# Order of VectorE's pieces inside an attention round: key counts, key shift and loser flags placed later or earlier

## The chip, the cores and the metric

The kernel runs on one core of one Trainium2 chip. The metric is the device time in microseconds of one execution, taken as the median of several runs. It is one transformer layer: attention with top-k pruning, then a mixture-of-experts part.

## The reference, cut to what matters

```python
mod = (silu(c) @ wmod).reshape(4, 6, 1, -1)            # sa, ca, ga, sb, cb, gb; ga and gb kept away from 0
h = layernorm(x) * (1 + ca) + sa                       # x: (4, 1024, 256)
q, k, v = (keep_largest(h @ w.T) for w in (wq, wk, wv))  # 16 heads of 16; of 16 features only the largest |.| stays
s = q @ k.T / 4, causal                                # per head, 1024 x 1024
s = keep the 64 largest of each row, the others -inf (ties: the lower key first)
x = x + ga * (softmax(s) @ v) @ wo.T
h = layernorm(x) * (1 + cb) + sb
g = softmax(h @ router_w + router_b)                   # 8 experts, each takes its 512 best tokens
x = x + gb * sum over experts of (relu(tok @ w1 + b1) @ w2 + b2) * g
```

Since only one feature of a query and one of a key survives, a score is a single product. Which keys belong to the 64 largest can be told by counting: `left` counts, along the keys, how many with the same feature and sign have gone by, and a row's kept keys are found by comparing ranks with counts.

## The kernel before, in words

The attention part goes in 16 **rounds** (`for gi in range(GA)`), each one batch `b` and one group `g` of four heads. A round's scores are computed in nine **units** (`UNITS`), each a piece of the 1024 x 1024 plane for four heads. TensorE computes `scores(gi, u)` (L424, L430, L435) into a ring of three pairs of PSUM banks (`begin`, `f_free`), ScalarE takes the exponential (`exps`, L947) into `p_buf`, and TensorE multiplies with the values (`pv`, L457) into PSUM bank 6. Bank 7 (`m_begin`, `f_mfree`) is used in turn by small results: turned key and query rows (`rows`, L376), `zero_rank` (L384 to L386), `own_key` (L392), `lost` (L400, L401), turned outputs (`turn_back`, L504), modulation rows (L517). Each of them waits until the one before has been emptied.

Units 1 and 4 hold the first 128 keys, among which the last of the 64 kept ones are decided: TensorE computes `chosen` (L448, L451) into two further ring buffers, and VectorE compares, `mask(gi, c, a)` (L1280), which needs the unit's exponentials and frees the ring buffer. `scores(gi, 5)` needs the buffer of `mask(gi, 1, 0)`.

In every round but the last, VectorE also prepares the next round's (`n = gi + 1`) keys and queries:

- `key_counts(n)` (L1221, L1223): which keys are zero, and the scan over all 1024 keys; it releases TensorE's `zero_rank(n)` by `f_cnr`.
- `keys(n)` (L1231 to L1244): the running maximum of the keys, their marks, the largest key `k_max` (L1241), and last the keys shifted by it (L1243, L1244), which releases `own_key(n)` by `f_kp`.
- `queries(n)` (L1249 to L1251), releases `lost(n)` by `f_uq`.
- `zero_rank(n)` (L1256, L1259), `losers(n)` (L1266), `negatives(n)` (L1272) empty bank 7 after TensorE's `zero_rank`, `own_key` and `lost`.

Other pieces on VectorE are `out_rows_of` (L1285 to L1288, divides the outputs and empties bank 7), and the next batch's work: `norm_stats` (L1168), `normalize` (L1178), `modulate` (L1188) and, four times in each round with g of 1 or 2 of the first three batches (`tiles`: rounds 1, 2, 5, 6, 9, 10), `one_feature` (L1198, L1203), which ScalarE's `evict_y` (L921) feeds and GpSimd's `keep` (L789, L790) follows; `feature_limits` (L1208 to L1215) in rounds 3, 7, 11. The batch before is finished in the next batch's rounds: `gate_weights`, `take_weights`, `take_mod`, `residual` (g = 0), `second_norm` (rounds 7, 11, 13). GpSimd further does `stage` (L769) and `tri` (L779, the triangle of units 2, 3 and 8, which `pv` of these units waits for).

The order on every engine is written out by hand, and each engine works its list strictly in order. So a piece that waits holds back all behind it. VectorE's order in a round stands in the loop at the end of its block (L1421 to L1494); TensorE's, ScalarE's and GpSimd's in theirs.

Of the kernel before, what the change touches and what calls it, by code (L numbers as in the profile page):

```python
# [32 lines left out]
def build_kernel(nc, x, wq, wk, wv, wo, router_w, router_b, w1, b1, w2, b2, c, wmod, out):  # L33
    with ExitStack() as ctx:
# [74 lines left out]
        def sf(name, shape, dt=F32):  # L109
            return fst.enter_context(nc.sbuf_tensor(name, shape, dt))  # L110
# [38 lines left out]
        kd = sf("kd", [P, 2, T])  # L149
# [89 lines left out]
        def full_of(u):  # L239
            return f_full[ring_at[u] % 3], ring_at[u] // 3 + 1  # L240
# [7 lines left out]
        def p_of(gi, u):  # L248
            return p_buf[:, (NU * gi + u) % PB]
# [34 lines left out]
        with nc.Block() as blk:  # L284
# [762 lines left out]
            def _(dve):  # L1047
# [133 lines left out]
                def modulate(b, half):  # L1181
                    u = ("T", b, half)
                    dve.wait_ge(*full_of(u))
                    v = ("Y", b - 1, NT - 1 if b > 1 else 3) if half == 0 else ("Y", b, 3)
                    if b:
                        dve.wait_ge(*full_of(v))
                    for k in range(KD):
                        m = dve.tensor_scalar(h_of(b, half)[:, k, :], buf(u)[:, k, :], mod_t[:, 1, k, b:b + 1], mod_t[:, 0, k, b:b + 1],  # L1188
                                              ALU.mult, ALU.add)
                    dve.drain().then_inc(free_of(u)[0], 1)  # L1190
                    dve.nop().then_inc(f_hT, 1)
                    dve.nop().then_inc(f_xfree, 1)

                def one_feature(b, t):
                    i = NT * b + t
                    dve.wait_ge(f_yev, i + 1)
                    y_abs, y_val, y_one = y_of(b, t)
                    dve.tensor_reduce(y_mx[:, b % 2, t, :], y_abs, AX.X, ALU.max)  # L1198
                    dve.drain()
                    if y_turn(b, t) > 0:  # L1200
                        dve.wait_ge(f_keep, y_turn(b, t))
                        dve.wait_ge(f_cnt, y_turn(b, t))
                    dve.tensor_tensor(y_one, y_abs,  # L1203
                                      y_mx[:, b % 2, t, :].unsqueeze(2).to_broadcast([P, 3 * NH, HD]),
                                      ALU.is_equal).then_inc(f_one, 1)
# [21 lines left out]
                def keys(n):  # L1227
                    par = n % 2
                    kx = kd[:, par, :]

                    dve.tensor_tensor_scan(mx[:, :], kx[:, 0:512], kx[:, 0:512], 0.0, ALU.max, ALU.max)  # L1231
                    dve.tensor_reduce(k_max1[:, :], kx[:, 512:T], AX.X, ALU.max)
                    dve.tensor_scalar(k_far[:, :], k_not[:, :], -FAR, None, ALU.mult)
                    dve.tensor_tensor(n_lo[:, :], n_lo[:, :], left[:, T - 1:T], ALU.min)
                    dve.scalar_tensor_tensor(kb[:, :], k_not[:, 0:P], FAR, kx[:, 0:P], ALU.mult, ALU.add)
                    dve.scalar_tensor_tensor(k_one[:, :, :], kx[:, 0:P].unsqueeze(1).to_broadcast([P, HG, P]), 0.0,
                                             onesz[:, :, :], ALU.is_gt, ALU.mult)
                    dve.scalar_tensor_tensor(k_opp[:, :, :], ks[:, par, :].unsqueeze(1).to_broadcast([P, HG, P]), 0.0,
                                             onesz[:, :, :], ALU.is_lt, ALU.mult)
                    dve.drain()  # L1240
                    dve.tensor_tensor(k_max[:, :], mx[:, 511:512], k_max1[:, :], ALU.max)  # L1241
                    dve.drain()
                    dve.tensor_scalar(ks[:, par, :], ks[:, par, :], k_max[:, :], None, ALU.subtract)  # L1243
                    dve.scalar_tensor_tensor(kx, kx, k_max[:, :], k_far[:, :], ALU.subtract, ALU.add).then_inc(f_kp, 1)  # L1244
# [30 lines left out]
                def mask(gi, c, a):  # L1275
                    u = ("Z", gi, c, a)
                    dve.wait_ge(*free_of(("S", gi, FIRST[c], a)))
                    dve.wait_ge(*full_of(u))
                    pb = p_of(gi, FIRST[c])[:, 2 * a:2 * a + 2, :]
                    dve.scalar_tensor_tensor(pb, buf(u), 1.0, pb, ALU.is_gt, ALU.mult).then_inc(free_of(u)[0], 1)  # L1280

                def out_rows_of(gi, c):
                    m_full(("O", gi, c))
                    o4 = ps[:, 7, :].rearrange("p (q h d) -> p q h d", q=4, h=HG)
                    dve.tensor_tensor(z_lo[:, :, :], z_lo[:, :, :], o4[:, :, :, HD], ALU.min)  # L1285
                    dve.reciprocal(o_inv[:, :, :], o4[:, :, :, HD])
                    dve.drain()
                    dve.tensor_tensor(o_tok[:, 4 * c:4 * c + 4, heads(gi % NG), :], o4[:, :, :, 0:HD],  # L1288
                                      o_inv[:, :, :].unsqueeze(3).to_broadcast([P, 4, HG, HD]), ALU.mult).then_inc(f_mfree, 1)
                    if gi % NG == NG - 1:  # L1290
                        dve.drain().then_inc(f_otok, 1)
# [129 lines left out]
                for gi in range(GA):  # L1421
                    b, g = divmod(gi, NG)
                    n = gi + 1
                    more, pre, post = n < GA, b + 1 < B, b > 0
                    tiles = pre and g in (1, 2)
                    t0 = 4 * (g - 1)

                    if g == 0 and post:
                        gate_weights(b - 1)
                        take_weights(b - 1)  # L1430
                    if gi == GA - 1:
                        gate_weights(b)
                        take_weights(b)
                    mask(gi, 0, 0)
                    mask(gi, 0, 1)
                    if gi == 0:
                        router_constants()
                        feature_limits(0)
                        finish_mod()
                    if tiles:  # L1440
                        one_feature(b + 1, t0)
                    if g == 0 and pre:
                        norm_stats(b + 1, 0)
                    if post and g == norm_group(b - 1):
                        second_norm(b - 1, 0)
                    if gi:
                        out_rows_of(gi - 1, 1)
                    if more:
                        key_counts(n)
                    if g == 0 and pre:  # L1450
                        normalize(b + 1, 0)
                    if tiles:
                        one_feature(b + 1, t0 + 1)
                    mask(gi, 1, 0)
                    mask(gi, 1, 1)
                    if post and g == norm_group(b - 1):
                        second_norm(b - 1, 1)
                    if g == 1 and pre:
                        norm_stats(b + 1, 1)
                    if more:  # L1460
                        keys(n)
                    if tiles:
                        one_feature(b + 1, t0 + 2)
                    out_rows_of(gi, 0)
                    if g == 0 and post:
                        take_mod(b - 1)
                    if gi == GA - 1:
                        take_mod(b)
                    if more:
                        queries(n)  # L1470
                    if g == 0 and post:
                        residual(b - 1, 0)
                    if more:
                        zero_rank(n)
                    if g == 1 and pre:
                        normalize(b + 1, 1)
                    if g == 0 and pre:
                        modulate(b + 1, 0)
                    if tiles:
                        one_feature(b + 1, t0 + 3)  # L1480
                    if g == 3 and pre:
                        feature_limits(b + 1)
                    if more:
                        losers(n)
                    if g == 0 and post:
                        residual(b - 1, 1)
                    if g == 1 and pre:
                        modulate(b + 1, 1)
                    if post and g == norm_group(b - 1):
                        router_max(b - 1, (0, 1))  # L1490
                    if more:
                        negatives(n)
                    if post and g == norm_group(b - 1):
                        router_share(b - 1, (0, 1))  # L1494
# [761 lines left out]
```

## Time and profile before

| | |
|---|---|
| median of 3 runs | 1086.58 us (1085.47 to 1089.87) |
| profiled execution, its own time | 1082.71 us |
| its span | 1080.8 us |
| TensorE matmul busy | 918.9 us (85%) |
| VectorE busy | 660.8 us (61%) |
| ScalarE busy | 480.0 us (44%) |
| GpSimd busy | 272.0 us (25%) |
| mean granted TensorE clock | 0.916 |

The span runs from the first to the last instruction; the execution's own time has 1.9 us around it. The attention rounds lie between about 65 us and 740 us, the experts behind them. The rows further down are from timelines: start, duration, engine, line, operation, tiles, count, and in brackets how long the engine had been idle before and what ended it. Rows of one kind that follow each other are merged, so that the duration is that of the whole run of them.

### The profile page before, as it was taken

Reading aid. Unit: us, or ns where it says so; the run is one execution under the profiler, and the core shown is the slowest. Engines: PE = TensorE matmul, PEld = TensorE weight load, DVE = VectorE, ACT = ScalarE, POOL = GpSimd, SP = SyncE. Lnnn points to the kernel's source line nnn. Section 1 sums busy time; section 2 is a strip of 40 time slices with the busy share of each in tenths; the row PEclk is TensorE's granted clock in tenths of the full one; section 3 lists DMA queues with packets and bytes.
Section 4 is the critical chain, followed back from the end, with each engine's and each line's share of the span. In section 5 each row is a group of like instructions: output and inputs, shape, how many; then the busy total and the mean of one; then the engine's idle time right before and its main releaser. Section 6 shows DMA issues by size and latency. Waiting matters only on the chain. (4 is left out here: it accounts for less than half of the span.)

```text
span 1080.8 us, 17735 instructions
## 1 busy us (share of the span) xinstructions
PE 918.9 (85%) x6760; PEld 503.2 (47%) x6760; DVE 660.8 (61%) x1454; ACT 480.0 (44%) x631; POOL 272.0 (25%) x404
## 2 busy tenths in 40 slices
PE   6778999888999888999989999985015999999995
PEld 4533444344444453544435535334003766666664
DVE  6757767566678657586684683634685455543441
ACT  2635667663667745476765475551000122222110
POOL 3503222321222402232221200010004333334222
PEclk9779999999999989999998998996555999999998
DMA  4000000000100011100002102001822134442111
GB/s 153 4 1 21 1 21 2 1 1 1 60 20 1 1 47 34 60 1 2 2 1 80 38 4 80 1 20 40 294 99 54 39 107 115 107 113 40 20 20 20
DMA packets 34856, 46.60 MB, mean 43 GB/s; under 512 B 2184, under 2 KB 30928, under 8 KB 34640
## 3 DMA queue, kind: packets, MB, share of 16 engines
q1 hardware_dynamic: 28624, 36.89, 10.2%
q0 software_dynamic: 6144, 8.52, 4.9%
q8 instruction: 57, 0.93, 0.4%
q14 instruction: 31, 0.25, 0.1%
HBM read 32.69 MB, written 12.72 MB: 42 GB/s over the span
## 5 line engine op out<-in xcount | busy, mean ns | idle before, releaser
L947 ACT ACTIVATE p_buf<-ps 128x1024 f32<-128x1024 f32 x288 | 279.4, 1023 | 181.0 <-PE ps L424 96.5
L424 PE MATMUL ps<-qx,kd 32*128 32x512 f32 (+3 forms) x1280 | 146.8, 535 | 29.8 <-DVE p_buf L1280 26.1
L457 PE MATMUL ps<-p_buf,vv 128*17 128x512 f32 (+3 forms) x1664 | 156.3, 477 | 0.0
L2089 ACT ACTIVATE h_t<-ps,b_t 128x512 f32<-128x512 f32 x64 | 44.0, 687 | 247.6 <-PE ps L2029 247.6
L1280 DVE SCALAR_TENSOR_TENSOR p_buf<-ps,p_buf 128x1024 f32<-128x1024 f32 x64 | 76.7, 1220 | 76.7 <-ACT p_buf L947 63.7
L2029 PE MATMUL ps<-tok_t,w_sb 128*128 128x512 f32 x256 | 113.8, 603 | 0.0
L2039 PE MATMUL ps<-w_sb,h_t 128*128 128x256 f32 x512 | 112.5, 380 | 0.8 <-ACT h_t L2089 0.8
L779 POOL TENSOR_SCALAR_AFFINE_SELECT p_buf<-p_buf 128x512 f32<-128x512 f32 x64 | 42.0, 670 | 272.4 <-ACT p_buf L947 269.7
L2039 PEld LDWEIGHTS ps<-w_sb,h_t 128*128 128x128 f32 x512 | 96.6, 190 | 15.3 <-ACT h_t L2089 1.6
L424 PEld LDWEIGHTS ps<-qx,kd 32*128 32x128 f32 x1280 | 55.1, 191 | 71.7 <-issue 56.2
L365 PE MATMUL ps<-w_t,h_t 128*128 128x512 f32 (+1 forms) x224 | 78.8, 496 | 0.8 <-ACT w_t L889 0.8
L789 POOL TENSOR_TENSOR qk<-y_val,y_one 128x512 f32<-128x512 f32 x28 | 32.4, 1159 | 179.2 <-DVE y_one L1203 179.2
L2029 PEld LDWEIGHTS ps<-tok_t,w_sb 128*128 128x128 f32 x256 | 49.0, 193 | 59.0 <-issue 58.7
L1988 POOL DMA_INDIRECT out_dram<-ctr,ids x32 | 50.8, 1587 | 95.9 <-issue 95.9
L457 PEld LDWEIGHTS ps<-p_buf,vv 128*17 128x17 f32 x1664 | 34.3, 97 | 60.3 <-issue 46.2
L365 PEld LDWEIGHTS ps<-w_t,h_t 128*128 128x128 f32 x224 | 40.4, 190 | 40.8 <-issue 39.3
L2141 DVE TENSOR_TENSOR eo<-ps,b_sb 128x256 f32<-128x256 f32 x32 | 13.6, 425 | 72.1 <-PE ps L2039 68.6
L921 ACT ACTIVATE y_abs<-ps 128x768 f32<-128x768 f32 x28 | 22.7, 811 | 47.9 <-PE ps L365 45.9
L2127 DVE SCALAR_TENSOR_TENSOR gbk<-gb_sb,of_b,gbk 128x256 f32<-128x256 f32 x96 | 40.1, 480 | 1.8
L1977 POOL DMA_INDIRECT tok<-h_table,ids x32 | 35.2, 1099 | 23.2 <-issue 22.0
L1198 DVE TENSOR_REDUCE y_mx<-y_abs 128x48 f32<-128x768 f32 x28 | 26.7, 952 | 22.9 <-ACT y_abs L921 22.6
L1223 DVE TENSOR_TENSOR_SCAN left<-k_not,minus 128x1024 bf16<-128x1024 bf16 x15 | 39.8, 2656 | 1.1
(291 smaller groups left out, 1406.2 us busy)
## 6 DMA issues: line engine op xcount, KB each, us to landing
w_sb<-in_L_ffn_w_dram SPq DMA_DIRECT2D x16, 1024.0 KB, 9.0
h_table<-xr SPq DMA_DIRECT2D x3, 1056.0 KB, 4.6
x_in<-in_L_attn_x_dram SPq DMA_DIRECT2D x6, 512.0 KB, 4.0
out_dram<-xr SPq DMA_DIRECT2D x3, 1024.0 KB, 5.2
xr<-in_L_attn_x_dram SPq DMA_DIRECT2D x3, 1024.0 KB, 5.7
h_table<-xr SPq DMA_DIRECT2D x2, 528.0 KB, 3.1
xr<-in_L_attn_x_dram SPq DMA_DIRECT2D x2, 512.0 KB, 5.4
p_buf<-in_L_wmod_dram SPq DMA_DIRECT2D x1, 1024.0 KB, 8.8
```

Of the source, the lines that this page charges most:

```text
L365: m = pe.matmul(buf(u)[:, bank, 0:n], src[:, k, (t % 4) * P:(t % 4 + 1) * P], w_t[:, k, lo:lo + n], start=k == 0, stop=k == KD - 1)
L424: m = pe.matmul(o, key, qx[r, par, t0:t0 + w], start=True, stop=not early)
L457: m = pe.matmul(ps[32 * h:32 * h + HD + 1, 6, o:o + w], vv[:, (gi // NG) % 2, i, HG * (gi % NG) + h, :], p_of(gi, u)[:, h, lo:lo + w], sta ...
L779: m = pool.affine_select(p, p, [[0, HG], [1, P]], ALU.is_ge, 0.0, base=0, channel_multiplier=-1)
L947: act.activation(p_of(gi, u)[:, 2 * a:2 * a + 2, :], buf(w), ACT.Exp, scale=0.25).then_inc(free_of(w)[0], 1)
L1223: dve.tensor_tensor_scan(left[:, :], k_not[:, :], minus1[:, :].to_broadcast([P, T]), TOPK + 0.5, ALU.add, ALU.add)
L1280: dve.scalar_tensor_tensor(pb, buf(u), 1.0, pb, ALU.is_gt, ALU.mult).then_inc(free_of(u)[0], 1)
L1988: pool.indirect_dma_start(out_rows, bass.IndirectOffsetOnAxis(ids[:, e, k:k + 1], 0), ctr[:, e % 2, k, :], None, compute_op=ALU.add).then_ ...
L2029: m = pe.matmul(ps[:, L1_BANKS[f % 3], :], w1_sb[:, e % WB, k, f * P:(f + 1) * P], tok_t[:, e % 2, k, :], start=k == 0, stop=k == KD - 1)
L2039: m = pe.matmul(ps[:, 4 + q % 2, 0:D], h1_t[:, f, q * P:(q + 1) * P], w2_sb[:, e % WB, f, :], start=f == 0, stop=f == FO - 1)
L2089: act.activation(h1_t[:, f, :], ps[:, L1_BANKS[f % 3], :], ACT.Relu, bias=b1_t[:, e * FO + f:e * FO + f + 1]).then_inc(s_h1, 1)
L2127: dve.scalar_tensor_tensor(gbk[:, a, q, :], gb_sb[:, b, :], of_b[:, e, q, b:b + 1], gbk[:, a, q, :], ALU.mult, ALU.add)
```

## The change

Only the order of VectorE's list changes. `keys(n)` is cut in two: its last two instructions (with the drain before them) become `keys_shifted(n)`. `key_counts(n)` and `normalize(b + 1, 0)` now stand behind the second `one_feature` and the two comparisons of unit 4; `out_rows_of(gi, 0)` stands between `keys(n)` and `keys_shifted(n)`, and ahead of the third `one_feature`; `losers(n)` stands ahead of the fourth `one_feature` and of `feature_limits`.

```diff
@@ def keys(n)
                     dve.drain()
                     dve.tensor_tensor(k_max[:, :], mx[:, 511:512], k_max1[:, :], ALU.max)
+
+                def keys_shifted(n):
+                    par = n % 2
+                    kx = kd[:, par, :]
                     dve.drain()
                     dve.tensor_scalar(ks[:, par, :], ks[:, par, :], k_max[:, :], None, ALU.subtract)
                     dve.scalar_tensor_tensor(kx, kx, k_max[:, :], k_far[:, :], ALU.subtract, ALU.add).then_inc(f_kp, 1)
@@ the loop over the rounds
                     if gi:
                         out_rows_of(gi - 1, 1)
+                    if tiles:
+                        one_feature(b + 1, t0 + 1)
+                    mask(gi, 1, 0)
+                    mask(gi, 1, 1)
                     if more:
                         key_counts(n)
                     if g == 0 and pre:
                         normalize(b + 1, 0)
-                    if tiles:
-                        one_feature(b + 1, t0 + 1)
-                    mask(gi, 1, 0)
-                    mask(gi, 1, 1)
                     if post and g == norm_group(b - 1):
                         second_norm(b - 1, 1)
                     if g == 1 and pre:
                         norm_stats(b + 1, 1)
                     if more:
                         keys(n)
+                    out_rows_of(gi, 0)
+                    if more:
+                        keys_shifted(n)
                     if tiles:
                         one_feature(b + 1, t0 + 2)
-                    out_rows_of(gi, 0)
...
                     if g == 0 and pre:
                         modulate(b + 1, 0)
+                    if more:
+                        losers(n)
                     if tiles:
                         one_feature(b + 1, t0 + 3)
                     if g == 3 and pre:
                         feature_limits(b + 1)
-                    if more:
-                        losers(n)
```

## Rows read from the trace of the kernel before

**Rows 1.** The page, busy time of TensorE: us, share, instructions.

```profile
PE   918.9 (85%) x6760; PEld 503.2 (47%) x6760; DVE 660.8 (61%) x1454; ACT 480.0 (44%) x631; POOL 272.0 (25%) x404
```

**Rows 2.** Sums of waits: who waited for whom, us in total, times, longest.

```profile
PE ps L424 <- DVE p_buf L1280: 26.1, 16, 3.9
```

**Rows 3.** Timeline of TensorE in round 3 (rank products, scores of unit 5, bank-7 steps).

```profile
207.11 0.89 PE L448 MATMUL ps<-uq,wk_r 32*128 32x512 bf16 x4
...
210.20 1.14 PE L424 MATMUL ps<-qx,kd 32*128 32x512 f32 x8 [1.61 <-DVE p_buf L1280]
...
217.31 0.23 PE L384 MATMUL ps<-left,partner 128*128 128x128 bf16 x1 [0.25 <-DVE o_tok L1288]
...
219.89 1.16 PE L392 MATMUL ps<-kb,k_one 128*128 128x128 f32 x8 [0.18 <-DVE z_rank L1256]
...
223.18 0.23 PE L400 MATMUL ps<-upto,lw 128*128 128x128 bf16 x1 [1.16 <-DVE lw L1266]
```

**Rows 4.** Timeline of ScalarE in round 3, exponentials of unit 4.

```profile
206.53 1.94 ACT L947 ACTIVATE p_buf<-ps 128x1024 f32<-128x1024 f32 x2 [0.80 <-PE ps L424]
```

**Rows 5.** Timeline of VectorE in round 3.

```profile
204.42 0.17 DVE L1285 TENSOR_TENSOR z_lo<-z_lo,ps 128x16 f32<-128x16 f32 x1 [3.75 <-PE ps L504]
...
205.17 0.68 DVE L1221 TENSOR_SCALAR k_not<-kd 128x1024 bf16<-128x1024 f32 x1
205.93 2.72 DVE L1223 TENSOR_TENSOR_SCAN left<-k_not,minus 128x1024 bf16<-128x1024 bf16 x1
208.83 2.36 DVE L1280 SCALAR_TENSOR_TENSOR p_buf<-ps,p_buf 128x1024 f32<-128x1024 f32 x2 [0.19 <-issue]
211.10 1.22 DVE L1231 TENSOR_TENSOR_SCAN mx<-kd 128x512 f32<-128x512 f32 x1
...
215.02 0.29 DVE L1243 TENSOR_SCALAR ks<-ks,k_max 128x128 f32<-128x128 f32 x1
...
216.42 0.16 DVE L1285 TENSOR_TENSOR z_lo<-z_lo,ps 128x16 f32<-128x16 f32 x1
...
217.40 0.75 DVE L1249 SCALAR_TENSOR_TENSOR qm<-mx,k_max,qx 128x512 bf16<-128x512 f32 x1
...
219.54 0.29 DVE L1256 TENSOR_SCALAR z_rank<-ps 128x128 f32<-128x128 f32 x1
...
220.80 0.36 DVE L1208 TENSOR_REDUCE y_ext<-y_mx 128x1 f32<-128x256 f32 x1
...
222.00 1.13 DVE L1266 SCALAR_TENSOR_TENSOR lw<-ps,y_mx,tie 128x128 bf16<-128x128 f32 x4
```

**Rows 6.** Timeline of VectorE in round 14, `losers`.

```profile
689.13 1.13 DVE L1266 SCALAR_TENSOR_TENSOR lw<-ps,y_mx,tie 128x128 bf16<-128x128 f32 x4 [1.33 <-PE ps L392]
```

**Rows 7.** Timeline of VectorE in round 1, second `one_feature` and the comparisons.

```profile
123.99 0.95 DVE L1198 TENSOR_REDUCE y_mx<-y_abs 128x48 f32<-128x768 f32 x1 [0.38 <-ACT y_abs L921]
...
125.96 2.35 DVE L1280 SCALAR_TENSOR_TENSOR p_buf<-ps,p_buf 128x1024 f32<-128x1024 f32 x2
```

**Rows 8.** Timelines at the end of round 2: GpSimd's triangle, TensorE's unit 8 products.

```profile
193.90 1.22 POOL L779 TENSOR_SCALAR_AFFINE_SELECT p_buf<-p_buf 128x512 f32<-128x512 f32 x2
...
196.82 1.06 PE L457 MATMUL ps<-p_buf,vv 128*17 128x384 f32 x16
```

**Rows 9.** Timelines: `normalize` in rounds 1 and 4, TensorE's waits in round 4.

```profile
142.68 1.28 DVE L1178 TENSOR_SCALAR x_in<-x_in,mv,rstd 128x256 f32<-128x256 f32 x4
...
241.65 2.28 DVE L1178 TENSOR_SCALAR x_in<-x_in,mv,rstd 128x256 f32<-128x256 f32 x4
...
246.34 1.54 PE L424 MATMUL ps<-qx,kd 32*128 32x512 f32 x8 [3.91 <-DVE p_buf L1280]
...
254.68 1.12 PE L517 MATMUL ps<-mod_rows,pick_b 4*128 4x512 f32 x2
```

**Rows 10.** Busy time by stretch: engines' us, TensorE's granted clock behind POOL's.

```profile
127.00:131.00 4.00, 3.67 (x16) 1.31 (x20) 3.85 (x12) 2.17 (x3) 1.52 (x3) 0.57 0.00 0
```

## The prediction

> **What bounds the kernel now.** I read the busy times, then the sums of waits, then the timelines of TensorE, VectorE, ScalarE and GpSimd through the sixteen rounds (a round is one pass of `for gi in range(GA)`: one batch, four heads). TensorE is busy 918.9 us of 1080.8 [rows 1], so in the attention part an edit counts only through what TensorE waits for. The wait to be attacked is plain: `scores(gi, 5)` needs the ring buffer that unit 4's comparison `mask(gi, 1, 0)` frees, and over 16 rounds it cost 26.1 us [rows 2]. Round 3 shows why. TensorE began the rank products at 207.11 and the next scores only at 210.20, 1.61 us idle [rows 3]; ScalarE's exponentials of unit 4 began at 206.53, two in 1.94 us [rows 4]. VectorE had run `key_counts` from 205.17 and could compare only at 208.83 [rows 5]. So the comparison was 1.2 us late (it could have run at about 207.6, when the first exponential and the first rank product are there).
>
> The same rows show a second thing. After the comparison VectorE works without a hole from 208.83 to 223.1, and in this stretch TensorE stops three more times for it: `zero_rank` at 217.31, `own_key` at 219.89, `lost` at 223.18 (1.16 us idle) [rows 3, 5]. They use one PSUM bank in turn, so each waits for VectorE to empty the one before. The late half of a round is VectorE's; the early half has its holes, 3.75 us in front of `out_rows_of(gi-1, 1)` among them [rows 5].
>
> **The change, part by part.** No instruction is added or removed and no DMA is moved; SP's and GpSimd's own lists stay. Only VectorE's order changes.
>
> (a) `key_counts` goes behind the two comparisons. It takes 3.5 us (205.17 to 208.65, two instructions and two drains) [rows 5]. Before, 2.3 to 3 us of it filled time in which VectorE would have waited for the comparison; now those stay empty and all 3.5 us lie in the busy half. The comparison comes 1.2 us sooner, the work behind it is 3.5 us longer.
>
> (b) The two shifting instructions go behind `out_rows_of(gi, 0)`. They take 1.4 us (215.02 to 216.42), the output rows 0.9 [rows 5]. Hence `zero_rank` on TensorE is spared these 1.4 us, but `own_key` needs `queries` and VectorE's `zero_rank` behind both, and gains nothing.
>
> (c) `losers` goes ahead of the fourth `one_feature` and of `feature_limits`. This takes 1.2 us (220.80 to 222.00) out of the path to `lost` in rounds 3, 7 and 11 [rows 5], and 1.97 us (123.99 to 125.96, one `one_feature` [rows 7]) in the six tile rounds.
>
> Now by round, measured at `lost`, the last thing TensorE needs of VectorE in a round.
>
> *Round 3.* Comparisons 207.65 to 210.0, counts to 213.5, keys (3.9, from 211.10 to 215.02) to 217.4, output rows to 218.1: `zero_rank` at 218.15 instead of 217.31. Shift to 219.6, queries (2.1) to 221.9, rank out 222.2: `own_key` at 222.25 instead of 219.89, +2.36. It takes 1.1, `losers` 1.1 more, `lost` at about 224.6 instead of 223.18: **+1.4**. `feature_limits` is then behind it, and there is time: TensorE is in the next unit 0.
> *Rounds 7 and 11* are alike with the second normalisation in between: **+1.2** each. *Round 13* has no `feature_limits` to move: **+2.35**. *Round 14* likewise, but there `losers` had waited 1.33 us for `own_key` [rows 6], which absorbs half: **+1.25**. Together 7.4.
>
> *Rounds 1, 5, 9* (features and the other half's statistics). Here the comparison is held by the second `one_feature`, which waits for ScalarE (0.38 us idle, 123.99) [rows 7], so taking the counts away frees nothing: the 0.72 us wait in these six rounds stays. The path to `lost` becomes 3.5 longer by (a) and 1.97 shorter by (c), 1.5; taken as **+1.45** each, since in round 5 `lost` waited a shade for this path already. Together 4.35.
>
> *Rounds 2, 6, 10.* VectorE has 2 to 3 us of holes behind the comparison, so `lost` moves by −0.3 to +0.35. But the fourth `one_feature` now comes 2.7 to 3.3 us later, and behind it GpSimd has `keep`, `stage` and the triangle of unit 8, which ended at 195.12, 1.7 us before TensorE's products of unit 8 at 196.82 [rows 8]. The cover of 1.7 us is gone and 1.0 to 1.3 are late: **+1.05, +1.65, +1.65**, 4.35.
>
> *Round 0.* The wait of 3.06 us shrinks, the counts and `normalize` stand behind. **+1.2**, with `normalize` at 1.2 us. In front of the comparison it took 2.28 for its four tiles in round 4 and only 1.28 in round 1 [rows 9]; in the slow one GpSimd was copying (`stage`), in the fast one not, and at its new place it is not. If it kept 2.28, rounds 0, 4 and 8 would each be 1.1 worse. The Trainium skill (GPSIMD Engine Reference, 1. Specifications) says that GpSimd shares its SBUF interface with VectorE's two-port and two-input instructions; by that rule the moved piece gets faster, and the rows agree.
>
> *Rounds 4 and 8.* TensorE waits 3.91 us here [rows 9]: counts and `normalize` both in front. TensorE could go on 3.4 us sooner (the rest of the 3.91 is the comparison itself). Then the fetch of the modulation rows waits for `out_rows_of(gi, 0)`: comparisons to 242.8, counts 246.3, normalising 247.5, keys 251.4, output rows 252.1, against 254.68 [rows 9]. Behind that, projection and residual give the pace as before: **−2.5** each, −5.
> *Round 12* has no `normalize`; its modulation rows come at the same time, **0**; round 15 has none of the moved pieces, 0.
>
> Sum: 7.4 + 4.35 + 4.35 + 1.2 − 5 = **+12.3 us**.
>
> (d) The clock, the one term the trace doesn't show for the new order. After the wait of round 1 TensorE's mean grant over 127 to 131 was 0.57, the 1.2 GHz level, for 3.4 us [rows 10]; I count one behind this wait in eight of the sixteen rounds (the scores there take up to twice as long: 1.54 in round 4 against 1.14 in round 3 [rows 3, 9]). One costs half its length, 1.7 us, unless TensorE waits for VectorE anyway. My sum hides them behind VectorE's path. Bounds: 0 (all stay hidden), and 11 rounds × 1.7 = +18.7 (in each of the 11 rounds that get longer, the new waits make one in the open). I take one more in the open, +1.7, because most new waits are followed at once by another that would cover it. The Trainium skill (TensorE: Matmul & The Clock Gate, Part 1) has the gate follow how busy the array has lately been; by that rule waits moved from one place to two in a round are no better than one, which speaks against the change.
>
> So **+14 us**: 1082.71 + 14 = 1096.7 for an execution like the profiled one. The three runs have their median at 1086.58, 3.9 above the profiled execution, and I give the time against it: **1100.6 us**.
>
> **The rivals.**
> 1. *Forecast*: VectorE's busy half grows by the counts and TensorE loses there more than it wins at unit 4. For it: three waits in that half already. Chance 0.60.
> 2. *The clock in the open*: as 1, with low stretches behind most `zero_rank` and `own_key` waits: +12.3 and 8 to 18.7, 1107 to 1117. Against it: the wait of 1.61 us in round 3 brought no low stretch (the eight products behind it took 1.14 us in all [rows 3]). By the Trainium skill's rule on the gate, cited above, this would be the outcome. Chance 0.18.
> 3. *It wins* (the other side): the comparison sits on the path of every round and the late half has room that I overlook, so the waits are simply gone: 2.6 in round 0, 1.2 in five rounds, 3.4 in rounds 4 and 8, 1.3 in round 12, 16.7 us less, 1070. It decides if `own_key` in round 3 comes no later than 11.1 us after the comparison's start, which it does now (208.83 to 219.89) [rows 3, 5]. Against it: that distance is filled with VectorE's work already. Chance 0.10.
> 4. *A wash*: moving `losers` and the output rows ahead gives back what the counts cost, because `lost` and not `own_key` is what TensorE needs; the six tile rounds then cost nothing and the sum is about +3.5. 1086 to 1092. Chance 0.12.
>
> **How the numbers follow.** About 0.5%, 5.4 us, is what a measurement of this kernel can tell from no change. Cases 1 and 2 are slower (0.78), 3 is faster (0.10), 4 the same (0.12). The range goes from the upper half of the wash, 1089, to the middle of the clock's case, 1113.
>
> **What would show it.** Right: the wait of `scores` for L1280 falls from 26.1 to about 10 us; new waits of L384 (2 to 4 us in rounds 0, 3, 4, 7) and L392 (1 to 2 us in most rounds); in rounds 2, 6 and 10 TensorE's unit 8 products wait for GpSimd about 1 us; rounds 4 and 8 shorter. Wrong: L392 without waits, or VectorE with holes between comparison and `losers` in the plain rounds; or low-clock stretches behind the new waits in most rounds (then case 2).

## The result: 1.4% slower, and the profile after

| | before | after |
|---|---|---|
| median | 1087.55 us (1085.47 to 1089.87) | 1102.93 us (1100.37 to 1104.32) |
| profiled execution, its own time | 1082.71 us | 1104.06 us |
| its span | 1080.8 us | 1102.2 us |

Four runs of each; ratio 1.0139, interval 1.0113 to 1.0166. The medians lie 15.4 us apart, the two profiled executions 21.4: the one of before was 4.8 us under the median of its runs and faster than each of them, the one after 1.1 us over its own. So what is read from the two traces below is up to 6 us larger than what the medians show. Slower executions of the kernel before have the lower mean grant (1079.91 us at 0.917, 1089.24 us at 0.907). The lines of before are now 4 higher from L1243 on: comparison L1284, output rows L1289 to L1292, shift L1247 and L1248, `zero_rank` L1260, `losers` L1270.

The page of the kernel after, busy times, to hold against [rows 1]:

```profile
PE 925.6 (84%) x6760; PEld 507.7 (46%) x6760; DVE 655.5 (59%) x1454; ACT 481.6 (44%) x631; POOL 264.4 (24%) x404
```

The instructions are the same. TensorE needs 6.7 us more for its own (925.6 instead of 918.9), so more of them ran at the low clock; the rest of the 21.4 us went into waits. Sums of waits of the kernel after, TensorE, 65 to 765 us (total, times, longest), against [rows 2]:

```profile
PE ps L384 <- DVE o_tok L1292: 19.0, 9, 3.2
PE ps L392 <- DVE z_rank L1260: 15.0, 10, 2.1
PE ps L424 <- DVE p_buf L1284: 9.5, 16, 1.1
PE ps L517 <- DVE o_tok L1292: 4.9, 3, 2.1
PE ps L457 <- POOL p_buf L779: 3.1, 3, 1.0
```

The wait that was attacked fell from 26.1 to 9.5 us. In its place stand 15.0 at `own_key`, where there had been 0.5, 19.0 at `zero_rank` instead of 4.7, 4.9 at the modulation rows and 3.1 at GpSimd's triangle. Round 3 shows how, TensorE's timeline of the kernel after, against [rows 3]:

```profile
215.86 0.89 PE L448 MATMUL ps<-uq,wk_r 32*128 32x512 bf16 x4
217.73 1.14 PE L424 MATMUL ps<-qx,kd 32*128 32x512 f32 x8 [0.39 <-DVE p_buf L1284]
...
226.45 0.23 PE L384 MATMUL ps<-left,partner 128*128 128x128 bf16 x1 [1.87 <-DVE o_tok L1292]
...
230.46 2.08 PE L392 MATMUL ps<-kb,k_one 128*128 128x128 f32 x8 [0.67 <-DVE z_rank L1260]
...
234.31 0.29 PE L400 MATMUL ps<-upto,lw 128*128 128x128 bf16 x1
```

VectorE's timeline of the same round, kernel after, against [rows 5]:

```profile
213.17 0.17 DVE L1289 TENSOR_TENSOR z_lo<-z_lo,ps 128x16 f32<-128x16 f32 x1 [3.75 <-PE ps L504]
...
216.36 2.36 DVE L1284 SCALAR_TENSOR_TENSOR p_buf<-ps,p_buf 128x1024 f32<-128x1024 f32 x2 [2.35 <-ACT p_buf L947]
218.63 0.68 DVE L1221 TENSOR_SCALAR k_not<-kd 128x1024 bf16<-128x1024 f32 x1
219.39 2.29 DVE L1223 TENSOR_TENSOR_SCAN left<-k_not,minus 128x1024 bf16<-128x1024 bf16 x1
221.80 1.23 DVE L1231 TENSOR_TENSOR_SCAN mx<-kd 128x512 f32<-128x512 f32 x1
```

VectorE now idles 2.35 us in front of the comparison, where it had counted before, and has the counts between comparison and keys. From the comparison's start to `zero_rank` it is 10.1 us (forecast 10.5, before 8.5), to `own_key` 14.1 (forecast 14.6, before 11.1), to `lost` 17.95 (before 14.35; forecast 16.95).

Read at `lost` (from one round's to the next, after minus before):

| rounds | forecast | measured |
|---|---|---|
| 0 | +1.2 | +2.3 |
| 3, 7, 11, 13, 14 | +7.4 | +10.7 |
| 1, 5, 9 | +4.35 | +8.5 |
| 2, 6, 10 | +4.35 | +4.3 |
| 4, 8 | −5 | −1.75 |
| 12 | 0 | −1.8 |
| sum | +12.3 | +22.2 |

Two things have to be known for this table. TensorE's waits for the triangle, 1.05 us each, which the forecast counts in rounds 2, 6 and 10, stand behind `lost` (in round 2 at 205.58, `lost` at 198.11), so the table has them a round later. Put where the forecast has them, the second row is +7.6 measured against +7.4, and the fourth +7.4 against +4.35. And 1.3 of the +2.3 in round 0 lie in front of everything that was moved (last section).

### The profile page after: what moved, and what is told of

It reads as the page before. It is cut to its first block and busy times, and to the rows that moved or that the text cites. A ratio compares the mean times of both kernels' runs of the same rounds, so it can differ in the third digit from the quotient of the medians.

```text
span 1102.2 us, 17735 instructions
## 1 busy us (share of the span) xinstructions
PE 925.6 (84%) x6760; PEld 507.7 (46%) x6760; DVE 655.5 (59%) x1454; ACT 481.6 (44%) x631; POOL 264.4 (24%) x404
## 5 line engine op out<-in xcount | busy, mean ns | idle before, releaser
L457 PE MATMUL ps<-p_buf,vv 128*17 128x512 f32 (+3 forms) x1664 | 158.5, 482 | 3.1 <-POOL p_buf L779 3.1
L1284 DVE SCALAR_TENSOR_TENSOR p_buf<-ps,p_buf 128x1024 f32<-128x1024 f32 x64 | 76.8, 1222 | 97.3 <-ACT p_buf L947 82.1
L789 POOL TENSOR_TENSOR qk<-y_val,y_one 128x512 f32<-128x512 f32 x28 | 35.1, 1254 | 186.2 <-DVE y_one L1203 186.2
L457 PEld LDWEIGHTS ps<-p_buf,vv 128*17 128x17 f32 x1664 | 34.2, 97 | 60.3 <-issue 43.1
L424 PE MATMUL ps<-qx,ks 32*128 32x512 f32 x256 | 37.4, 654 | 3.9 <-ACT p_buf L947 3.9
```

The lines of the kernel that those rows point to most:

```text
L424: m = pe.matmul(o, key, qx[r, par, t0:t0 + w], start=True, stop=not early)
L457: m = pe.matmul(ps[32 * h:32 * h + HD + 1, 6, o:o + w], vv[:, (gi // NG) % 2, i, HG * (gi % NG) + h, :], p_of(gi, u)[:, h, lo:lo + w], sta ...
L789: pool.tensor_tensor(qk[:, t], y_val[:, 0:2 * NH], y_one[:, 0:2 * NH], ALU.mult)
```

## The experiments

A ratio is always to the kernel before on the same chip, with its interval. The chips differ a little (the kernel before took 1082.35 us on one and 1087.55 on another), so runs are compared by their ratios. All runs return the same result as the kernel before.

### The moves one by one

**Counts and normalising alone.** The kernel before, with this edit only:

```diff
-                    if more:
-                        key_counts(n)
-                    if g == 0 and pre:
-                        normalize(b + 1, 0)
...
                     mask(gi, 1, 1)
+                    if more:
+                        key_counts(n)
+                    if g == 0 and pre:
+                        normalize(b + 1, 0)
```

> Part (a) alone: key_counts and normalize behind the comparisons of unit 4, output rows and losers where they were before. Theory (the counts' 3.5 us lie in VectorE's busy half): slower than the changed kernel, since (b) and (c) had paid part of it back: lost comes 1.2 us later in rounds 3, 7 and 11, up to 2 us later in rounds 1, 5 and 9, about 0.4 in rounds 2, 6 and 10, and output rows 1.5 us later in rounds 4 and 8; about 1116 us, 13 us over the changed kernel. Rival (the loss is low-clock stretches, the order behind the comparisons doesn't matter): within 4 us of the changed kernel, 1099 to 1107.

Measured: 1132.49 us, ratio 1.0409 (1.0364 to 1.0454). The direction is the theory's, the size is not: 46 us lost instead of 29. Sums of waits, TensorE:

```profile
PE ps L384 <- DVE o_tok L1288: 40.5, 12, 4.7
PE ps L517 <- DVE o_tok L1288: 9.6, 3, 3.6
PE ps L424 <- DVE p_buf L1280: 9.5, 16, 1.1
```

The comparison's wait is 9.5 here too, so this gain comes from this piece alone; and nothing waits at `own_key`. The loss stands at `zero_rank`, in waits of up to 4.7 us.

**Output rows ahead of the shift, and `losers` earlier, alone.** The kernel before, with `keys` cut in two as in the change, and with these edits only:

```diff
                         keys(n)
+                    out_rows_of(gi, 0)
+                    if more:
+                        keys_shifted(n)
                     if tiles:
                         one_feature(b + 1, t0 + 2)
-                    out_rows_of(gi, 0)
...
+                    if more:
+                        losers(n)
                     if tiles:
                         one_feature(b + 1, t0 + 3)
                     if g == 3 and pre:
                         feature_limits(b + 1)
-                    if more:
-                        losers(n)
```

> Parts (b) and (c) alone: the output rows ahead of the key shift, losers ahead of the fourth one_feature and feature_limits; key_counts and normalize stay in front of the comparisons. Theory: a gain over the kernel before, as the waits of zero_rank (4.7 us in the sum of waits) and of lost (4.8) go: about 8 us, 1079.7 us; the wait of the scores for the comparison stays at about 26 us. Rival (b and c are harmful or nothing: GpSimd's triangle late, or another bank-7 step takes over): within 3 us of 1087.5.

Measured: 1087.57 us, ratio 1.0009 (0.9990 to 1.0027), a miss: nothing is won. VectorE's timeline, round 0 of this kernel:

```profile
94.83 0.16 DVE L1241 TENSOR_TENSOR k_max<-mx,k_max 128x1 f32<-128x1 f32 x1
96.67 0.17 DVE L1289 TENSOR_TENSOR z_lo<-z_lo,ps 128x16 f32<-128x16 f32 x1 [1.68 <-PE ps L504]
...
97.60 0.29 DVE L1247 TENSOR_SCALAR ks<-ks,k_max 128x128 f32<-128x128 f32 x1
...
101.14 0.29 DVE L1260 TENSOR_SCALAR z_rank<-ps 128x128 f32<-128x128 f32 x1
```

Its comparison starts at 88.90, so `zero_rank`'s result comes 12.2 us behind it; in the kernel before it was 10.7. The output rows wait 1.68 us for TensorE to turn them, and the shift, which was ready, stands behind that wait. Where VectorE is not late, this move only makes a hole. `lost` of round 0 comes 1.0 us later by it.

**`losers` earlier, alone** (the second hunk above).

> Part (c) alone on the kernel before: losers ahead of the fourth one_feature and of feature_limits. Theory: lost comes 1.2 us earlier in rounds 3, 7 and 11 and 0.9 in rounds 2, 6 and 10, where the products of unit 8 then wait 1 us for GpSimd's triangle and lose it again: 1083 us, 3.5 below the kernel before. Rival (the moves b and c together gained nothing because c is worth nothing): 1086.4.

Measured: 1079.27 us, ratio 0.9975 (0.9957 to 0.9992). The small gain is there. Against the run before, the output-row move is what took it away, some 0.3 points (the two intervals just touch). The hole of round 0 is 1 us of that. In the sums of waits the move takes away 7.7 us at `zero_rank` and brings 9.6 us at `own_key`, ten waits where there had been none.

**The changed kernel without the output-row move:**

```diff
                         keys(n)
-                    out_rows_of(gi, 0)
                     if more:
                         keys_shifted(n)
                     if tiles:
                         one_feature(b + 1, t0 + 2)
+                    out_rows_of(gi, 0)
```

> The changed kernel without part (b): keys shifted at once, output rows behind. Theory: zero_rank waits 1.4 us longer in nine rounds, but own_key waits for VectorE's zero_rank, which comes at the same time, so this is hidden there; in rounds 4, 8 and 12 the modulation rows wait 1.4 us longer, 4.2 in all: 1107 us. If (b) instead puts a hole into VectorE's list (the shift waiting behind output rows that TensorE has not turned yet), that hole goes in the rounds where VectorE is ahead and the time falls: 1100 us or less.

Measured: 1135.60 us, ratio 1.0497 (1.0465 to 1.0529). Neither theory has this. The move that costs 0.3% with the counts in front saves 3.6% here. TensorE in round 3 of this kernel:

```profile
230.57 0.23 PE L384 MATMUL ps<-left,partner 128*128 128x128 bf16 x1 [3.42 <-DVE o_tok L1292]
...
231.83 1.92 PE L424 MATMUL ps<-qx,kd 32*128 32x384 f32 x16
...
233.68 2.00 PE L392 MATMUL ps<-kb,k_one 128*128 128x128 f32 x8
```

One wait of 3.42 us instead of the 1.87 and 0.67 above, and `own_key`'s eight products take 2.00 us, the 1.2 GHz level. But they took 2.08 in the changed kernel too, and round 3 is as long in both. The difference shows in other rounds, here 14. The changed kernel:

```profile
706.22 0.23 PE L384 MATMUL ps<-left,partner 128*128 128x128 bf16 x1 [1.87 <-DVE o_tok L1292]
...
710.14 1.16 PE L392 MATMUL ps<-kb,k_one 128*128 128x128 f32 x8 [1.52 <-DVE z_rank L1260]
```

and the one without the output-row move:

```profile
738.10 0.29 PE L384 MATMUL ps<-left,partner 128*128 128x128 bf16 x1 [3.42 <-DVE o_tok L1292]
...
742.39 1.94 PE L392 MATMUL ps<-kb,k_one 128*128 128x128 f32 x8
```

The waits add up to the same, 3.39 and 3.42 us; the one long wait is followed by the low level, the two short ones are not, and the round is 3.4 us longer. In round 13 too the waits add up alike (4.52 and 4.55 us), and it is 3.3 us longer without the move. Is it the clock? The next run asks.

### Is it the clock?

**The same kernel with TensorE kept busy.** Fourteen matmuls that compute nothing (into a ring buffer whose content is overwritten later) stand in front of `zero_rank` in ten rounds and in front of the modulation rows:

```diff
+                def fill(count):
+                    i = len(ring_at)
+                    pe.wait_ge(f_free[i % 3], i // 3)
+                    for j in range(count):
+                        pe.matmul(ps[:, 2 * (i % 3) + j % 2, :], ...)
...
                     if g == 0 and post:
+                        fill(14)
                         spread_mod(b - 1)
...
                     scores(gi, 7)
+                    if more and gi not in (2, 4, 6, 8, 12):
+                        fill(14)
```

> The changed kernel without (b), as before, plus 14 idle matmuls (128 x 512, bf16, into a ring buffer that the next scores overwrite, about 3 us) on TensorE in front of zero_rank in the rounds that waited 3 to 4.7 us there, and in front of the modulation rows in rounds 4, 8 and 12. Nothing else changes, VectorE's list neither. Theory (the extra loss without (b) is the clock: one long wait of TensorE is followed by a stretch at 1.2 GHz, two short ones often not): low stretches fall from about 116 us to 60, the ratio from 1.050 to 1.025 or less. Rival (the output rows being late is itself the cost, the clock follows along): ratio 1.045 or more.

Measured: 1108.22 us, ratio 1.0222 (1.0162 to 1.0282). Windows view over 85 to 740 us (busy us of the five engines, then the granted clock, DMA share, GB/s), first without the filling:

```profile
85.00:740.00 655.00, 577.01 (x4651) 273.36 (x4647) 411.21 (x756) 373.43 (x473) 126.75 (x170) 0.92 0.06 20
```

and with it:

```profile
85.00:740.00 655.00, 610.31 (x5102) 285.27 (x5103) 422.43 (x778) 389.79 (x491) 128.79 (x174) 0.98 0.06 20
```

TensorE in round 3 of the filled kernel:

```profile
224.34 3.19 PE L568 MATMUL ps<-onesz,identb 128*128 128x512 bf16 x14
227.83 0.23 PE L384 MATMUL ps<-left,partner 128*128 128x128 bf16 x1 [0.29 <-DVE o_tok L1302]
...
230.41 1.16 PE L392 MATMUL ps<-kb,k_one 128*128 128x128 f32 x8 [0.18 <-DVE z_rank L1270]
```

The grant rises from 0.92 to 0.98, `own_key` is back at 1.16 us, and 2.75 points of the 5 are gone with no change of VectorE's order. The grant in steps of 1 us, added up from behind the start of the scores to the last `lost`, gives the time at the low level: 51 us in the kernel before, 61 in the changed one, 112 without the output-row move, 27 with the filling. Half of the 51 us between the second and the third is 26, of 31.6 us by which the two spans differ. So most of what the output-row move saves in the changed kernel is clock. That this comes from cutting one long wait into two short ones is what rounds 13 and 14 suggest; over all rounds the waits also got shorter (`zero_rank`, `own_key` and modulation rows together 51.6 us without the move, 38.9 with it), and the runs don't part the two. The Trainium skill (TensorE: Matmul & The Clock Gate, Part 1) has the gate follow how busy the array has been lately; these rows agree. What the prediction concluded from it, that two waits are no better than one, does not hold in rounds 13 and 14.

**The changed kernel itself, filled in the same way.**

> The changed kernel with the same idle matmuls. Its waits of zero_rank are 1 to 3 us, so 14 of them are longer than the wait in rounds 1, 5 and 9 and shorter elsewhere. Theory: VectorE's path sets the pace, so at most what the clock costs comes back, about 61 us of low stretches now: ratio 1.005 to 1.012 against 1.0139; not below 1.0. Rival (the whole loss of the change is the clock): ratio 0.99 to 1.0.

Measured: 1101.79 us, ratio 1.0157 (1.0111 to 1.0203). This lies above what both theories gave. Its grant over 85 to 740 us is 0.99, and by the ratio it can't be told from the changed kernel (1.0139). In round 3 its `lost` comes 15.1 us behind the scores of unit 5 instead of 16.6, so there the filling pays; rounds 6, 10 and 12 are 1.5 to 3.1 us longer than in the changed kernel. (The execution with the trace was at the fast end, 1098.41 us; two of the four took 1105.) Against the filled kernel without the output-row move (1.0222) the move is worth 0.65 points, with overlapping intervals, where it was 3.6 unfilled: again most of its worth is clock. The loss of the change is there at nearly full clock, so it isn't only the clock's. The filling itself takes time where it is longer than the wait, so how much of the loss is clock this run can't say.

### Where the counts belong

**Counts back in front of the comparison**, everything else as changed:

```diff
                         out_rows_of(gi - 1, 1)
+                    if more:
+                        key_counts(n)
...
                     mask(gi, 1, 1)
-                    if more:
-                        key_counts(n)
```

> The changed kernel with one piece put back: key_counts(n) in front of the second one_feature and the comparisons, where it was before; normalize stays behind. Theory: the whole loss and more comes back, since the counts fill the hole in the early half again and only normalize (which held up the comparison in rounds 0, 4 and 8) has left it: 1071 us, 32 below the changed kernel and 16 below the one before; waits of zero_rank and own_key below 4 us together. Rival (the clock): only the low stretches behind the new waits go, 6 stretches of 3.4 us at half speed, so about 10 us below the changed kernel, 1093.

Measured: 1077.85 us, ratio 0.9924 (0.9904 to 0.9945): 2.15 points, some 23 us, below the changed kernel by this one step. It is faster than before because `normalize` stays behind the comparison: that is the only difference to the run with the last two moves (1.0009). `own_key` still waits, 10.0 us in all, where less than 4 was forecast.

**Counts back in front in the six tile rounds only:**

```diff
+                    if tiles:
+                        key_counts(n)
                     if tiles:
                         one_feature(b + 1, t0 + 1)
...
-                    if more:
+                    if more and not tiles:
                         key_counts(n)
```

> The changed kernel with key_counts put back in front of the comparisons in the six rounds with features only (1, 2, 5, 6, 9, 10). Theory by rounds: there the comparison waits for ScalarE's tile, so the counts in front cost nothing and the 8.7 us that I summed for these six rounds, with what the clock adds, come back: ratio 1.003 to 1.007. Rival (the loss lies in the rounds without features): 1.012 or more.

Measured: 1094.28 us, ratio 1.0067 (1.0045 to 1.0089). Half of the loss lies in the tile rounds (forecast: 8.7 of 12.3).

**Counts first of all**, ahead of `out_rows_of(gi - 1, 1)`, in the hole of 3.75 us, everything else as changed:

```diff
+                    if more:
+                        key_counts(n)
                     if gi:
                         out_rows_of(gi - 1, 1)
...
                     mask(gi, 1, 1)
-                    if more:
-                        key_counts(n)
```

> As the kernel with the counts in front, and key_counts(n) further ahead, before out_rows_of(gi - 1, 1), where VectorE idles 3.7 us in the rounds without features. Theory: the comparison of unit 4 comes up to 0.9 us sooner in about seven rounds, 5 us less than with the counts in front, 1066 us; the output rows come 2.8 us later there, which nothing waits for before the query rows. Rival: the output rows' delay holds bank 7, the query rows wait for it, and the gain is 0 or a loss of up to 1 us per round.

Measured: 1069.07 us, ratio 0.9837 (0.9806 to 0.9869). The comparison's wait is 12.0 us, and the late half has no counts.

**That, without the output-row move**, and with `losers` behind the fourth `one_feature` in rounds 2, 6 and 10 (the edit names round 14 too, which has no features):

```diff
                         keys(n)
-                    out_rows_of(gi, 0)
                     if more:
                         keys_shifted(n)
                     if tiles:
                         one_feature(b + 1, t0 + 2)
+                    out_rows_of(gi, 0)
...
-                    if more:
+                    if more and g != 2:
                         losers(n)
...
+                    if more and g == 2:
+                        losers(n)
```

> The kernel with the counts ahead of the output rows, now without (b), and with losers in its old place in rounds 2, 6, 10 and 14. Theory of the hole: in the rounds in which VectorE is ahead (0, 4, 8, 12) the shift no longer waits for the turned output, about 1 us in round 0, and rounds 2, 6, 10 lose the 1 us wait for GpSimd; rounds 5, 7 and 11 get a wait of zero_rank back. 1066 us against 1069. If output rows late is what counts: 1073.

Measured: 1059.58 us, ratio 0.9788 (0.9758 to 0.9817), the fastest of all and 2.1% below the kernel before. Sums of waits, TensorE, 65 to 735 us:

```profile
PE ps L424 <- DVE p_buf L1284: 12.0, 16, 1.4
PE ps L384 <- DVE o_tok L1292: 5.0, 6, 1.5
PE ps L400 <- DVE lw L1270: 3.8, 6, 0.9
```

VectorE in round 3 of it:

```profile
201.61 0.70 DVE L1221 TENSOR_SCALAR k_not<-kd 128x1024 bf16<-128x1024 f32 x1 [3.03 <-ACT kd L938]
202.39 2.29 DVE L1223 TENSOR_TENSOR_SCAN left<-k_not,minus 128x1024 bf16<-128x1024 bf16 x1
204.80 0.17 DVE L1289 TENSOR_TENSOR z_lo<-z_lo,ps 128x16 f32<-128x16 f32 x1
205.55 2.35 DVE L1284 SCALAR_TENSOR_TENSOR p_buf<-ps,p_buf 128x1024 f32<-128x1024 f32 x2
```

Counts and output rows are done just when the comparison can start. The waits of `own_key` and of the triangle are no longer in the list. The two edits against the run before this one were not tried apart, and the intervals of the two runs just overlap.

**The output-row move kept only in rounds 1, 5, 9 and 7, 11, 13**, otherwise as the run before:

```diff
+                    late_v = tiles and g == 1 or post and g == norm_group(b - 1)
+                    if late_v:
+                        out_rows_of(gi, 0)
                     if more:
                         keys_shifted(n)
                     if tiles:
                         one_feature(b + 1, t0 + 2)
-                    out_rows_of(gi, 0)
+                    if not late_v:
+                        out_rows_of(gi, 0)
```

> As the one before, but with (b) kept in rounds 1, 5, 9 and in those with the second normalisation (7, 11, 13), where VectorE is late when the output has been turned. Theory: the waits of zero_rank in 5, 7 and 11 go too: 1 to 3 us below it, 1064 us. Rival (own_key decides, zero_rank's wait is hidden): same as the one before, within 1.5 us.

Measured: 1061.51 us, ratio 0.9805 (0.9765 to 0.9845), which can't be told from the run before. With VectorE in time the move is worth nothing in either place.

## Why the prediction was right, and where its sizes were off

The forecast case 1 held: slower, 1102.93 us against 1100.6, by the mechanism named. That the time came so near is in part luck: +14 stands against +15.4 by the medians, but against +22.2 by the rows from which it was worked out, and there misses of both signs lie beside each other.

- **(a), the counts.** Confirmed. The comparison's wait fell to 9.5 us ("about 10"), waits of L384 of 1.9 to 3.2 us came in rounds 0, 3 and 7 as named (in round 4 it was the modulation rows that waited, 2.07), of L392 in ten rounds, and bringing the counts back in front recovers the loss (0.9924).
- **Rounds 3, 7 and their like.** The distances up to `own_key` came within half a us of the forecast (0.4 and 0.5 shorter). Not forecast: in rounds 3 and 7 `own_key` itself ran at the low level, 2.08 and 2.07 us instead of 1.16.
- **Rounds 2, 6, 10.** Half right. TensorE waits 3.1 us for the triangle in these three, as summed, and `losers` earlier is its cause (the wait has the same 3.1 with that edit alone). But `lost` was to move by −0.3 to +0.35 and moved by +2.45, +0.8 and +1.0: `own_key` waits there for VectorE, 1.05, 1.25 and 1.62 us, which the forecast took for holes on VectorE.
- **Round 12** was put at 0, its modulation rows "at the same time". They came 1.8 us sooner behind the `lost` before: the comparison's wait fell from 1.80 to 0.49 us, and TensorE was 3 us less at the low level in front of it.
- **`normalize` at its new place** took 1.39 us in round 4 instead of 2.28, near the 1.2 assumed.
- **Rounds 4 and 8.** The modulation rows came as forecast (11.4 us behind the comparison, forecast 11.7; 2.7 sooner behind the `lost` of round 3, forecast 2.5). But "projection and residual give the pace as before" failed. TensorE in round 4, kernel before:

```profile
255.73 3.72 PE L536 MATMUL ps<-wo_t,o_t 128*128 128x256 f32 x16
```

and after:

```profile
254.22 1.14 PE L424 MATMUL ps<-qx,kd 32*128 32x512 f32 x8 [0.49 <-DVE p_buf L1284]
...
263.10 1.12 PE L517 MATMUL ps<-mod_rows,pick_b 4*128 4x512 f32 x2 [2.07 <-DVE o_tok L1292]
264.15 5.41 PE L536 MATMUL ps<-wo_t,o_t 128*128 128x256 f32 x16
```

The projection behind the new wait runs slow: 5.41 instead of 3.72, in round 8 the same. Over 263 to 270 us the grant is 0.76; over 254 to 260 before it was 1.00. That is 1.7 us in each of the two rounds and turns −5 into −1.6; −1.75 was measured.
- **(d), the clock, is the term that was mis-sized.** It stood at +1.7, "most new waits are followed at once by another that would cover it". Low stretches did come behind the new waits in nine rounds (0, 1, 3, 4, 5, 7, 8, 9, 11), which the prediction itself had named as the sign of case 2. Windows view of the kernel after, round 1 and round 5:

```profile
149.00:153.00 4.00, 4.00 (x28) 2.64 (x24) 3.86 (x10) 1.74 (x3) 0.07 (x1) 0.57 0.00 0
323.00:327.00 4.00, 4.00 (x25) 2.42 (x24) 3.86 (x11) 1.81 (x2) 0.00 (x0) 0.57 0.02 6
```

Where they lie on the path they cost this, by rows of the profiled execution: projections 3.4, `own_key` in rounds 3 and 7 1.8, rounds 1, 5 and 9 3.6 (3 × 1.2, from round 1 below), together some 9 of the 22.2. TensorE in round 1 of the kernel after shows where it lay open:

```profile
147.66 1.16 PE L392 MATMUL ps<-kb,k_one 128*128 128x128 f32 x8 [2.14 <-DVE z_rank L1260]
148.75 1.52 PE L457 MATMUL ps<-p_buf,vv 128*17 128x512 f32 x8
150.19 1.97 PE L353 MATMUL ps<-ident,x_in 128*128 128x128 f32 x8
151.96 0.31 PE L400 MATMUL ps<-upto,lw 128*128 128x128 bf16 x1
```

Before, the products with the values and the turning behind them (L457, L353) took 1.05 and 1.09 us, together 2.1; now 3.5, and in rounds 5 and 9 3.6 and 3.7. They stand right in front of `lost`, where nothing hides them: `lost` comes 23.7 us behind the comparison's start, forecast 22.5. But these 9 us count new stretches only. Of the eight behind the comparison's wait, which the prediction had counted in the kernel before, one is left (round 2), so that the time at the low level rose only from 51 to 61 us, which is 5 us of TensorE's time. How much of the old stretches had been hidden, no run shows, so the clock's share of the loss stays open; both counts, 5 and 9 us, are estimates from these rows and lie above the 1.7 forecast. Case 2 (12.3 and at least 8, so +20.3) was met at its low end by the rows, +22.2, and missed by the medians, +15.4.
- **(b), the output-row move**, was costed at nothing, since `own_key` gains nothing. Right for `own_key`, wrong as a price: it is worth +0.3% with the counts in front, and −3.6% in the changed kernel, most of it clock. That it came out near nothing in the sum was not seen from a row.
- **Rivals 3 and 4** fell. The late half had no room, and the tile rounds cost half.
- **Two readings of the prediction were thin.** Against case 2 it held the wait of 1.61 us in round 3, with no low stretch behind it; in round 14 of the same kernel the same wait had one:

```profile
677.32 2.09 PE L424 MATMUL ps<-qx,kd 32*128 32x512 f32 x8 [1.61 <-DVE p_buf L1280]
```

The upper bound of (d) takes 11 rounds that get longer; by its own list there are 12, with round 0.
- **Open:** why the kernel with counts behind and `losers` earlier (1.0497) is slower than the one with the counts alone (1.0409), and how the loss divides into the clock and the rest.

## What to carry to other kernels

A wait that is removed by moving work behind it is paid for wherever that work now stands in front of a later dependant: look first for a hole ahead of the waiting piece (here the one in front of the earlier output rows), and only then behind it. The 2.1% of the fastest kernel come from three steps: `normalize` behind the comparison 0.85 points, the counts into the hole 0.9, the output rows and `losers` back 0.5. On TensorE two short waits can cost less than one long one, so price a new wait with the matmuls behind it, which may run at half clock. An early place in an in-order list helps only if the piece placed there is itself ready.

## What was not expected of the hardware

- One wait of 3.42 us (round 14) or 4.55 us (round 13) cost over 3 us more than nearly the same time in two waits, while in round 3 there was no such difference. Filling the long waits with idle matmuls raised the grant from 0.92 to 0.98 and took 2.75 points off the time, with VectorE's order untouched.
- The length of one wait doesn't tell whether the level falls. It fell behind 2.07 us (the projection, 5.41 instead of 3.72 us), behind 1.61 us in round 14 of the kernel before and behind 0.72 us in its round 1 [rows 10]; it stayed behind the 1.61 us of [rows 3].
- The same scan over 1024 keys took 2.29 us in the new place and 2.72 in the old [rows 5]. Likewise the query product of round 1, L1254, took this in the kernel after, VectorE's timeline:

```profile
144.41 2.18 DVE L1254 SCALAR_TENSOR_TENSOR uq<-qx,left 128x1024 bf16<-128x1024 f32 x1
```

and 1.22 us in the rounds without features. In the slow cases GpSimd was at work beside it; that this is the cause was only observed, not tried, and the scan of round 0 before took 2.29 us although GpSimd was busy beside it too.
- TensorE's first low stretch behind the start of the scores lasted 1.3 us longer in one profiled execution than in the other, with the same work and no moved piece before it. Ten of the thirteen profiled executions here have the long form, among the three with the short one is the kernel before. That it is chance is likely but not shown; a difference of profiled spans can hold that much.
